# Wv and Wo of each head merged into one matrix per layer in a six-layer local-attention stack run twice

## The reference, cut to what matters

```python
qkv = x @ Wqkv                       # 128 -> 3 * 1024
q, k, v = jnp.split(qkv, 3, -1)      # 16 heads of 64 each
q = l2norm(q) * qs; k = l2norm(k) * ksc          # then rotary tables on both
sim = jnp.einsum('bhwie,bhwje->bhwij', bq, bk2) * QK_SCALE   # 32 queries x 64 keys
attn = jax.nn.softmax(jnp.where(mask, -big, sim), -1)
out = jnp.einsum('bhwij,bhwje->bhwie', attn, bv2)
return out.transpose(0, 2, 1, 3).reshape(b, n, INNER) @ Wo   # 1024 -> 128
```

## Time and profile before

| what | value |
|---|---|
| median of 3 runs | 3281.72 us (3278.72 to 3283.54) |
| profiled execution, its span | 3281.1 us |
| PE busy | 3130.3 us, 95% |
| DVE busy | 2721.8 us, 83% |
| ACT busy | 2486.3 us, 76% |
| POOL busy | 2434.9 us, 74% |
| granted TensorE clock, mean | 0.992 |

### The profile page before, as it was taken

How to read it: one execution, slowest core, us unless ns; L and a number is a source line. 1 busy time by engine, 2 the same in 40 slices (tenths; PEclk the granted TensorE clock), 3 DMA queues, 4 the chain that set the end, 5 groups by cost and what they waited for, 6 DMA issues and landing times.

```text
span 3281.1 us, 120591 instructions
## 1 busy us (share of the span) xinstructions
PE 3130.3 (95%) x51702; PEld 2520.7 (77%) x51702; DVE 2721.8 (83%) x3169; ACT 2486.3 (76%) x3160; POOL 2434.9 (74%) x1229
## 2 busy tenths in 40 slices
PE   7999999999999999998888999999999999999999
PEld 5888888888888887875333788888788888888787
DVE  7887888888888888877999888888888888888886
ACT  5777777787777777777676777778777778778776
POOL 6787787776776776762999778778768768778664
PEclk8999999999999999999999999999999999999999
DMA  3333233233233332231000323323323323323222
GB/s 121 89 80 87 71 93 86 68 91 86 72 88 85 75 84 66 71 75 42 20 0 1 98 67 80 91 72 85 92 72 81 94 71 81 97 66 90 69 67 66
DMA packets 142300, 245.23 MB, mean 75 GB/s; under 512 B 32397, under 2 KB 34638, under 8 KB 141774
## 3 DMA queue, kind: packets, MB, share of 16 engines
q1 hardware_dynamic: 141774, 237.51, 28.5%
HBM read 35.01 MB, written 1.05 MB: 11 GB/s over the span
## 4 chain that ended last, share of the span: by engine, by line
PE 84%; issue 5%; DVE 5%; POOL 3%; ACT 3%; DMA 0%; SPq 0%; ACTq 0%; DVEq 0%; POOLq 0%
PE PS L283 16%; PE PS L407 12%; PE PS L427 8%; PE PS L352 8%; PE PS L215 8%; PE PS L217 7%; PE PS L216 7%; PE PS L564 4%; PE PS L506 2%; PE PS L508 2%; PE PS L507 2%; PE PS L362 2%; PE PS L450 2%; POOL ARENA L1893 2%; DVE ARENA L1706 2%
## 5 line engine op out<-in xcount | busy, mean ns | idle before, releaser
L283 PE MATMUL PS<-C,ARENA 128*128 128x128 f32 x4608 | 619.7, 278 | 38.4 <-ACT ARENA L1025 11.4
L1777 POOL TENSOR_TENSOR ARENA<-ARENA 128x1024 f32<-128x1024 f32 x192 | 470.5, 2451 | 235.3 <-DVE ARENA L1359 234.5
L1785 POOL TENSOR_TENSOR ARENA<-ARENA,RN 128x1024 f32<-128x1024 f32 x192 | 365.3, 1903 | 367.7 <-ACT RN L960 367.7
L283 PEld LDWEIGHTS PS<-C,ARENA 128*128 128x128 f32 x4608 | 512.4, 141 | 119.1 <-issue 77.8
L1025 ACT ACTIVATE ARENA<-PS 64x1024 f32<-64x1024 f32 x384 | 390.5, 1017 | 182.2 <-PE PS L283 180.0
L215 PE MATMUL PS<-WL,XH 128*128 128x512 f32 x1152 | 500.0, 434 | 8.4 <-POOL XL L1744 4.0
L1771 POOL TENSOR_TENSOR ARENA<-ARENA 128x1024 f32<-128x1024 f32 x192 | 456.2, 2376 | 7.0 <-DVE ARENA L1341 7.0
L217 PE MATMUL PS<-WH,XH 128*128 128x512 f32 x1152 | 454.7, 395 | 0.1
L216 PE MATMUL PS<-WH,XL 128*128 128x512 f32 x1152 | 452.2, 393 | 0.0
L407 PE MATMUL PS<-ARENA 128*64 128x64 f32 x12288 | 403.0, 224 | 27.4 <-DVE ARENA L1399 14.0
L407 PEld LDWEIGHTS PS<-ARENA 128*64 128x64 f32 x12288 | 376.7, 138 | 60.8 <-issue 60.8
(11 more groups left out here) (163 smaller groups left out, 6419.1 us busy)
## 6 DMA issues: line engine op xcount, KB each, us to landing
ARENA<-ARENA SPq DMA_DIRECT2D x1152, 128.0 KB, 2.4
ARENA<-ARENA SPq DMA_DIRECT2D x768, 64.0 KB, 2.1
ARENA<-in_wqkv SPq DMA_DIRECT2D x36, 512.0 KB, 5.4
ARENA<-in_wo SPq DMA_DIRECT2D x12, 512.0 KB, 3.8
ARENA<-in_w SPq DMA_DIRECT2D x12, 341.0 KB, 3.1
ARENA<-in_w SPq DMA_DIRECT2D x12, 192.0 KB, 4.6
X<-in_xT SPq DMA_DIRECT2D x4, 256.0 KB, 4.6
out<-X SPq DMA_DIRECT2D x1, 768.0 KB, 3.3
```

What stands on the lines that cost most here:

```text
L283: last = nc.tensor.transpose(PS[:, slot, 128 * j:128 * j + 128], src[:, 128 * j:128 * j + 128], ident)
L1777: nc.gpsimd.tensor_tensor(KN[n % 2], KN[n % 2], T2, ALU.add).then_inc(k_add, 1)
```

## The change

The host sends Wv transposed beside Wo (`wvo`). In the first stack, before each layer, the kernel multiplies the two factors of each head on PE (K = 64, 128 x 128 results), keeps the 2048 columns in `MS` and writes them to DRAM (`MD`); the second stack loads them from there. V becomes a projection of 2048 columns in two parts: `v_project_high` (slot 3, columns 1024 up) and `v_project_low` (slot 2). Four DMAs per tile spread 32 rows of 2048 onto 128 partitions of 512, so that partition 4*key + a holds 128 output columns for head 4g + a. The probabilities are stored key by key with four heads beside each other. The value products now use the transposed probabilities (128 x 32) as weights and the values (128 x 128) as moving side, and sum over the eight chunks of heads and keys in PSUM: 128 tokens x 128 output columns. `out_project` is gone; the result is copied out (128 x 128), and once a unit four transposes turn it, and the residual is added for 512 columns at once. Several steps change place: value products come before the q transposes, feed-forward centring before `v_project_low`, the variance product before the probabilities' transposes.

```diff
@@ PE
-            def v_project(n):
+            def v_project_high(n):
+                pe.wait_ge(w_lo[3], l0 + n // NT + 1)
+                after_tile(pe, sub_done, n - 1)
+                project(n, 3, 3, vb_done)
+            def v_project_low(n):
...
+                after_tile(pe, qT_ev, n)
+                project(n, 2, 2, va_done)
+            def merge_products(half):
+                wv, wo = (VO0[:, 0:1024], VO0[:, 1024:2048]) if half < 2 else (WS[:, 0:1024], WS[:, 1024:2048])
+                for g in range(4):
+                    w = slice(512 * (half % 2) + 128 * g, 512 * (half % 2) + 128 * g + 128)
+                    for u in range(2):
+                        a, b = 64 * u, 64 * u + 64
+                        last = nc.tensor.matmul(PS[:, 3, 512 * u + 128 * g:512 * u + 128 * g + 128], wv[a:b, w], wo[a:b, w],
+                                                start=True, stop=True, skip_group_check=True)
+                last.then_inc(mv_done, 1)
+            def merge_weights(n):
+                if r == 1 or not 0 <= n < N - NT or n % NT not in (5, 9):
+                    return
...
+                pe.wait_ge(vb_ev, n + 1)
+                merge_products(2 * l + n % NT // 9)
-            def value_products(n):
-                pt = PTS.rearrange("p (h w x) -> p h w x", h=8, w=4)
-                v2 = V2[n % 2].rearrange("p (w h d) -> p w h d", w=4, h=8)
...
+            def value_products(n, bank):
+                for i in range(8):
                     for win in range(4):
+                        k = win + i % 2 - 1
+                        v = V3[(n - 1) % 3] if k < 0 else V3[n % 3] if k == 3 else V4[n % 2][:, 512 * k:512 * k + 512]
+                        last = nc.tensor.matmul(
+                            PSB[32 * win:32 * win + 32, bank, 0:128], PTS[:, 128 * i + 32 * win:128 * i + 32 * win + 32],
+                            v[:, 128 * (i // 2):128 * (i // 2) + 128], start=i == 0, stop=i == 7, skip_group_check=True)
                 last.then_inc(pv_done, 1)
             def values(n):
                 pe.wait_ge(PT_ev, n0 + n + 1)
-                pe.wait_ge(v2_in[n % 2], 160 * ((n0 + n) // 2 + 1))
-                after_tile(pe, sub_done, s - 21)
+                pe.wait_ge(v_in[n % 2], 64 * ((n0 + n) // 2 + 1))
-            def out_products(n, bank):
-                w = WO[n // NT % 2]
-                for j in range(8):
-                    last = nc.tensor.matmul(PSB[:, bank, 0:128], w[:, 128 * j:128 * j + 128], OTS[:, 128 * j:128 * j + 128],
-                                            start=j == 0, stop=j == 7)
+            def out_products(u, bank):
+                for i, n in enumerate(unit_tiles(u)):
+                    last = nc.tensor.transpose(PSB[:, bank, 128 * i:128 * i + 128], OT4[:, 128 * (n % 4):128 * (n % 4) + 128], ident)
@@ PE loop
                 k_project(s - 19)
-                out_project(s - 23)
+                first_merge(s - 0)
+                out_transpose(s - 23)
+                values(s - 22)
                 q_transpose(s - 20)
-                values(s - 22)
+                v_project_high(s - 20)
                 k_transpose(s - 20)
+                merge_weights(s - 20)
...
                 q_project(s - 18)
-                v_project(s - 20)
+                ffn_centre(s - 23)
+                v_project_low(s - 20)
                 scores(s - 20)
+                ffn_variance(s - 23)
@@ ACT
-                act.activation(P.rearrange("p (h a s) -> p a h s", a=2, s=64),
-                               SB.rearrange("p (a h s) -> p a h s", a=2, s=64), ACT.Exp, scale=8.0).then_inc(exp_done, 1)
+                act.activation(by_groups(P), SB.rearrange("p (g a m) -> p g m a", g=4, a=4), ACT.Exp,
+                               scale=8.0).then_inc(exp_done, 1)
-                for par in range(2):
-                    a, b = 64 * par, 64 * par + 64
-                    last = act.activation(blocks[a:b, :, par, :], PS[a:b, slot, :].rearrange("p (b q) -> p b q", q=32), ACT.Copy)
+                act.activation(PTS, PS[:, slot, :], ACT.Copy).then_inc(PT_ev, 1)
-                act.activation(OTS, PS[:, 3, :], ACT.Copy).then_inc(oT_ev, 1)
+                act.activation(OT4[:, 128 * (n % 4):128 * (n % 4) + 128], PSB[:, bank, 0:128], ACT.Copy).then_inc(o_ev, 1)
@@ DVE
-                nc.vector.tensor_reduce(SM[:, n % 2, :], heads(P), AX.X, ALU.add).then_inc(sm_done, 1)
+                nc.vector.tensor_reduce(SM[:, n % 2, :].rearrange("p (g a) -> p g a", g=4), by_groups(P).rearrange("p g m a -> p g a m"), AX.X, ALU.add).then_inc(sm_done, 1)
+            if r == 0:
+                for t in range(2):
+                    dve.wait_ge(mv_done, t + 1)
+                    nc.vector.tensor_copy(MS[:, 1024 * t:1024 * t + 1024], PS[:, 3, :]).then_inc(mv_ev, 1)
@@ POOL
             def w_low_v(x):
                 if 0 <= x < N - NT and x % NT == NT - 1:
+                    low_weights(x // NT + 1, 3)
                     low_weights(x // NT + 1, 2)
-                nc.gpsimd.tensor_tensor(heads(P), heads(P), bc(RI[:, n % 2, :], 64), ALU.mult).then_inc(p_nrm, 1)
+                nc.gpsimd.tensor_tensor(
+                    by_groups(P), by_groups(P), RI[:, n % 2, :].rearrange("p (g a) -> p g a", g=4).unsqueeze(2)
+                    .broadcast_to([128, 4, 64, 4]), ALU.mult).then_inc(p_nrm, 1)
@@ SP
-                for par in range(2):
-                    a, c = 64 * par, slice(512 * par, 512 * par + 512)
...
+                for j in range(4):
+                    dst = V4[n % 2][:, 512 * j:512 * j + 512] if j < 3 else V3[n % 3]
+                    sp.dma_start(dst, VT[n % 2][32 * j:32 * j + 32, :]).then_inc(v_in[n % 2], 16)
```

More of the change, by code:

```diff
@@ L29, with build @@
 NM = 45
[L32 removed]
+def build(nc, xT, consts, wqk, wvo, w1, w2, lpar, qks, mpar, in_w, xp_w, dt_w, out_w, out):
     ctx = ExitStack()
@@ L132, in build, with unit_tiles @@
         SXT, RST, XCT = SQ[:, 0:512], SQ[:, 512:1024], T2[:, 0:512]
+        def unit_tiles(u):
+            return range(4 * u, 4 * u + 4) if u < UNITS - 2 else range(2 * u + N - 2 * UNITS, 2 * u + N - 2 * UNITS + 2)
         def unit(u):
@@ L598, in finish_tiles @@
                 transposes(0, KN[1], kT_done)
-                tile(oT_ev, 92)
-                tile(res_done, 91)
-                units(f_ln, u)
-                out_products(92, 2)
                 tile(q_nrm, 95)
@@ L605, in finish_tiles @@
                 transposes(2, QN[1], qT_done)
+                pe.wait_ge(v_in[1], 64 * ((n0 + 93) // 2 + 1))
+                tile(o_ev, 92)
+                units(f_ln, u)
+                value_products(93, 2)
                 tile(sub_done, 94)
-                pe.wait_ge(v2_in[1], 160 * ((n0 + 93) // 2 + 1))
-                value_products(93)
+                project(95, 3, 3, vb_done)
                 tile(qT_ev, 95)
@@ L1410, in row_sums, with unit_residual, residual @@
                 nc.vector.reciprocal(RI[:, n % 2, :], SM[:, n % 2, :]).then_inc(ri_done, 1)
-            def residual(n):
-                if not 0 <= n < N:
-                    return
-                q0 = 128 * (n % NT)
-                dve.wait_ge(wo_done, n0 + n + 1)
-                nc.vector.tensor_tensor(B[0:64, q0:q0 + 128], PSB[0:64, 2, 0:128], A[0:64, q0:q0 + 128], ALU.add)
-                nc.vector.tensor_tensor(B[64:128, q0 + 1:q0 + 129], PSB[64:128, 2, 0:128], A[64:128, q0 + 1:q0 + 129],
+            def unit_residual(u, bank):
+                q0, w, x = unit(u)
+                dve.wait_ge(oT_done, c0 + u + 1)
+                nc.vector.tensor_tensor(B[0:64, q0:q0 + w], PSB[0:64, bank, 0:w], A[0:64, q0:q0 + w], ALU.add)
+                nc.vector.tensor_tensor(B[64:128, q0 + 1:q0 + w + 1], PSB[64:128, bank, 0:w], A[64:128, q0 + 1:q0 + w + 1],
                                         ALU.add).then_inc(res_done, 1)
+            def residual(x):
+                if 0 <= x < N and x % 4 == 3:
+                    unit_residual(x // 4, 3)
             def normalise(u, bank):
@@ L1553, in vector_stack @@
             normalise(u, 3)
-            residual(92)
+            half_input(u)
             row_sums(94)
@@ L1557, in vector_stack @@
             subtract_max(95, 0)
-            residual(93)
-            half_input(u)
             row_sums(95)
@@ L1571, in vector_stack @@
                 keep_centred(dve, 1, 3)
-            residual(95)
+            unit_residual(u + 2, 7)
             half_input(u + 2)
@@ L1946, in sync_stack @@
+                for a, b in ((LP[:, :], lpar), (MP[:, :], mpar)):
                     sp.dma_start(a, b).then_inc(const_in, 16)
@@ L1952, in sync_stack @@
                 l, T = divmod(n, NT)
+                if r == 0 and n == 0:
+                    put_merged(0)
                 if l + 1 < NL and T == 2:
-                    for g in range(3):
+                    for g in range(2):
                         sp.wait_ge(w_lo[g], l0 + l + 1)
+                    if r == 0:
```

(9 more changed lines are left out.)

459 lines of the change are left out of this document (212 added, 247 removed).

## The result

The changed kernel takes 3288.4 us (median of 20 runs, 3281.3 to 3294.0) against 3283.4 us for the kernel before in the same session (20 runs, 3277.2 to 3286.9). The ratio is 1.0014 with a 95% interval of 1.0008 to 1.0020: some 5 us slower where 42 us less were forecast.

What follows compares the result with a forecast made beforehand. PE, busy 95% of the span, was taken to bound the kernel. Terms of -75, +25, -25, +14, +17 and +2 summed to -42 us, so 3240 us; the 8-in-10 range was 3195 to 3330.

Steps and rivals of the forecast that it cites:

- eaten by edges: Rival: slower value products, costlier layer borders and a late probabilities copy use up the gain; 3281 us, chance 0.13.
- PE's work, with the output transposes: PE over 192 steps: output products go, a second v projection comes, -75 us; four transposes a unit, +25.
- waits that go (14.0 and 11.4): PE's waits before the value products (14.0 us) and the transposes of q (11.4) disappear: -25 us in all.
- strided operands: New access patterns in row sums, exponentials and probabilities' scaling: 1.25 us added on their ring, under the slack, so 0.
- layer borders: Upper v projection waits for its weights' low part; PE stands 1.5 to 2 us at ten borders: +17 us.
- merges: Merging weights in the first stack: ten half layers of eight products, 1.4 us each with waiting: +14 us.
- The rival of groups that don't overlap: Rival: the value products' four column groups don't run fully side by side; at 2.5 us, 3345 us; chance 0.08.
- The exponentials have about 2 us before the row sums need them ..., so I cost their slowdown at 0 too: Exponentials on ACT, now reading 64 floats apart: any slowdown hides before the row sums need them, 0 us.
- The row sums: DVE's row sums, reading every fourth float, get 0.7 us longer and the scaling 0.55; under the slack, so 0.
- a slack of 1.57: Time that can be added for nothing to the 10.53 us ring over row sums and scaling, against PE's 12.10 step.
- The value products no longer wait for the row maximum to be subtracted ..., so the 14.0 us go: Value products, moved to slot 1, lose PE's 14.0 us wait for the subtraction; part of the -25 us.
- The slower rival: Rival: the ring over row sums and scaling becomes the bound, from 1.86 us added; middle 3320 us, chance 0.24.

Runs made afterwards that it cites:

- experiment 1: Changed kernel with exponentials and row sums both put back to reading SB's own order (output not the reference's): 3254.7 us, ratio 0.9909.
- Experiment 5: DVE's low part of the next layer's feed-forward weights moved behind the subtraction: 3268.7 us in the changed kernel, 3265.8 in the kernel before.

## Why the prediction was wrong

The forecast was 3240 us; the measured 3288.4 lies in the range (3195 to 3330), in the case called "eaten by edges", though not for its reasons. Step by step:

| step | forecast | measured |
|---|---|---|
| PE's work, with the output transposes | -50 | -48 (-36.8 in both stacks, with ten merges of 1.09 in it) |
| waits that go (14.0 and 11.4) | -25 | the first stayed (27.4 us before, 27.5 after); the 11.4 left the list |
| strided operands | 0 | +34 (experiment 1) |
| layer borders | +17 | +9 by removal, ten waits of 1.3 in the trace |
| merges | +14 | +5 by removing the work, up to 11 with the waits |
| start, middle and end | +2 | +2.4 |

- *PE's work: right.* Three times the 21.2 us of the four layers would be -63, but the first and last layers gain less: the whole second stack has 26.3. Value products start 1.89 us before what follows them (2.02 before; I took 1.95), where 64 of them one behind the other would take 7.1 us (an estimate from the 0.111 us of an output product), so four column groups do run side by side. The rival of groups that don't overlap is out, and with it its price:

```profile
1088.93 1.96 PE L428 MATMUL PS<-ARENA 128*32 128x128 f32 x64
1090.82 1.09 PE L327 MATMUL PS<-C,ARENA 128*128 128x128 f32 x8
```

- *"The exponentials have about 2 us before the row sums need them ..., so I cost their slowdown at 0 too": the step that failed.* I asked only who reads the exponentials' result, and found slack. I did not ask what is queued behind them on ACT: the small copy of the outputs, for which the transposes of k wait, then the copies of the transposes and of v. In a layer's step 14, where a weight split stands ahead, and in its step 4, where the subtraction comes late, the queue has no slack (gaps of 0.47 and 0.60 us before the transposes of k). I had no row for the size either and took none: it doubled. Price: 17 us alone, 34 with the row sums.
- *The row sums: size about right, effect not.* I took +0.7 us, it is +0.81; I took +0.55 for the scaling, it is 0. Together 0.81 against a slack of 1.57, and alone they cost only 6 us. But with the exponentials 1.05 us longer as well, the loaded steps are over their slack. The 1.57 us were worked out for a plain step, and there they held. By the Trainium skill, "Vector Engine (DVE) Microarchitecture Reference", section 5.2, the estimate for the row sums was 1.9 to 2.7 us; the trace agrees at its lower end (2.02 us).
- *"The value products no longer wait for the row maximum to be subtracted ..., so the 14.0 us go": failed.* The wait belongs to the slot which the scores filled, and the upper v projection writes into that slot. Its row in the order of the changed kernel already had `s_sub_done` among its waits. Who takes over a slot takes over its wait. Experiment 5 prices most of it at 15 us. The forecast had also read it too small: it is 27.4 us, since the six waits called "issue" belong to it, so even its own argument should have booked -27.
- *The borders were laid out right* (1.5 us of gap from start to start, 1.5 to 2 forecast), and what their removal gave was smaller than the sum of the gaps; that waits behind them took up the rest is my reading, no run shows it. *The merges* were oversized by 3 to 9 us.
- *The slower rival* named the right engines with the wrong member: its ring went over row sums and scaling, and would decide from 1.86 us added. The ring that did decide went over ACT's queue.

Two of these steps make the miss: 34 us for the patterns and 14 for the wait that stayed are 48, the distance from 3240 to 3288. That the other terms came out near the forecast in sum is partly luck. The 11.4 us of waits before the transposes of q left the list, but PE's idle time before all transposes did not fall (38.4 us before, 49.1 after), so they were no gain in full.

The profiles can be added up another way. PE's work without the merges is -48, the merges' own work +11, what lies around the stacks +2.4. Of the 41.4 us more of idle time 23 went when the patterns were put back; the border waits hold 12.7 and the waits of the merges 5.9. That makes +7, which is what the two spans differ by. The agreement is closer than it deserves, since these waits overlap: the merges' waits, for one, are 3.3 us with the patterns put back.

One more thing differs between the two. The granted clock was 0.989 over the changed kernel and 0.992 over the kernel before, and 0.97 against 0.99 in the last layer of the first stack. An estimate from the two means: PE stood at the lower of its two clocks (1.2 GHz) for some 72 us, against 53. It costs at most half of the 20 us between them and lies in PE's busy time above; no run separates it.

## What to carry to other kernels

When an edit changes the access pattern of an instruction, price its duration at twice until a row shows otherwise, and follow two paths from it: who reads its result, and who is queued behind it on its own engine. When a step moves into a buffer or slot, it inherits the waits of whoever used the slot before; read the waits of the new instruction in the order, not those of the old one. In a list of waits, look at the lines called "issue" too: here they hid half of the wait that mattered. If a layout needs a permutation, look for the one that keeps runs of some tens of elements and let the DMA, which here had time, do the interleaving.

## What the runs showed of the hardware

- ACT takes 2.10 us for 128 x 1024 floats read at a hop of 256 bytes and written in a run, 2.12 read in a run and written at a hop of 16 bytes, 2.08 with hops on both sides (256 and 512 bytes), and 1.05 to 1.07 with runs of 32 floats or more: each of the hops tried doubles it, and two cost no more than one.
- DVE's reduction of 128 x 1024 floats takes 1.21 us in runs of 32 or 64 and 2.02 at a hop of 16 bytes. POOL's product of two operands stays at 1.90 whether the small operand changes every 64 elements or at each one.
- 64 matmuls of 128 x 32 weights and 128 columns, four column groups accumulating in one bank, take 1.89 us from start to start.
